# Reading back the first choices' rows in ten loads of two blocks instead of six paired loads, at the end of a graph-attention and expert-layer kernel

## What is computed

```python
gate = jax.nn.softmax(xt @ Wg, axis=-1)
topv, topi = jax.lax.top_k(gate, K)                      # K = 2 of 8 experts
topv = topv / (jnp.sum(topv, axis=-1, keepdims=True) + 1e-06)
...
for e in range(E):
    h = jax.nn.gelu(xt @ W1[e] + b1[e], approximate=False)
    ye = h @ W2[e] + b2[e]
    out = out + ye * scores[:, e:e + 1]
...
x = x + ffn(layernorm(x))
```

## Time and profile before

| | us |
|---|---|
| median of three runs | 1333.1 (1332.76 to 1335.24) |
| the profiled execution, its own time | 1335.91 |
| its span, first to last instruction | 1334.2 |
| busy: PE, DVE, POOL, ACT | 1198.6, 1066.7, 772.1, 696.7 |
| the tiles of the experts | about 1105 to 1306 of the span |
| the sums and their stores | about 1306 to 1334 |

### The profile page before, as it was taken

The page is one execution under the profiler, slowest core; times in us unless marked ns, Lnnn a source line. Parts: engine busy times, 40 slices in busy tenths (PEclk is TensorE's granted clock), DMA queues, the critical chain, the costliest instruction groups (busy, mean ns, idle before and its releaser), DMA issues. The chain is left out here.

```text
span 1334.2 us, 23031 instructions
## 1 busy us (share of the span) xinstructions
PE 1198.6 (90%) x6584; PEld 844.4 (63%) x6585; DVE 1066.7 (80%) x2179; ACT 696.7 (52%) x1198; POOL 772.1 (58%) x859
## 2 busy tenths in 40 slices
PE   6999995999999999999994999999999747999985
PEld 1455554756666666666652888877777535777752
DVE  8999888999999999999988998888888992212216
ACT  5444433988898998989882000000100565555541
POOL 1201006776777777777727777777777704655541
PEclk9999996999999999999995999999999867999988
DMA  9134328998999999999958898888887763343478
GB/s 258 64 127 159 127 96 297 315 296 279 310 310 311 312 309 306 310 301 313 306 150 205 280 314 286 290 293 289 291 271 246 260 229 107 133 134 134 129 272 312
DMA packets 141838, 324.61 MB, mean 243 GB/s; under 512 B 30178, under 2 KB 46294, under 8 KB 141610
## 3 DMA queue, kind: packets, MB, share of 16 engines
q0 software_dynamic: 62816, 212.87, 49.1%
q1 hardware_dynamic: 76842, 109.42, 24.2%
q10 hardware_dynamic: 2080, 1.05, 0.3%
HBM read 257.35 MB, written 65.93 MB: 242 GB/s over the span
## 5 line engine op out<-in xcount | busy, mean ns | idle before, releaser
L1337 PE MATMUL m_ps<-msg,big 128*128 128x260 f32 x1344 | 304.8, 387 | 15.0 <-SPq L1148 14.7
L1337 PEld LDWEIGHTS m_ps<-msg,big 128*128 128x128 f32 x1344 | 254.2, 191 | 65.7 <-issue 27.8
L1188 POOL DMA_INDIRECT big<-he_d,target x234 | 237.5, 1015 | 71.3 <-issue 66.1
L952 PE MATMUL gs_ps<-hrs,hot_t 128*128 x672 | 245.0, 446 | 6.5 <-DVE hot_t L791 4.4
L1261 DVE TENSOR_TENSOR msg<-big 128x512 f32<-128x512 f32 x336 | 213.2, 689 | 40.8 <-DMA big<-he_d,target 39.3
L773 POOL DMA_INDIRECT x_sb<-table_d,target x186 | 192.6, 1035 | 77.0 <-issue 40.7
L1059 ACT ACTIVATE big<-big,raw_a 128x512 f32<-128x512 f32 x264 | 215.4, 816 | 8.8
L804 DVE TENSOR_TENSOR big<-big 128x512 f32<-128x512 f32 x264 | 179.8, 681 | 6.0 <-ACT big L1059 5.6
L1057 ACT ACTIVATE big<-d_ps 128x512 f32<-128x512 f32 x264 | 155.0, 587 | 49.1 <-PE d_ps L972 47.8
L798 DVE TENSOR_TENSOR x_sb<-x_sb,gs_ps 128x512 f32<-128x512 f32 x252 | 169.0, 678 | 14.2 <-PE gs_ps L952 7.3
L972 PE MATMUL d_ps<-ident,x_sb 128*128 128x128 f32 x1008 | 162.3, 284 | 4.1 <-DVE x_sb L798 3.3
(11 more groups left out here) (361 smaller groups left out, 2021.1 us busy)
## 6 DMA issues: line engine op xcount, KB each, us to landing
big<-early_d SPq DMA_DIRECT2D x84, 256.0 KB, 4.3
early_d<-x_sb SPq DMA_DIRECT2D x63, 256.0 KB
x_sb<-local_d SPq DMA_DIRECT2D x84, 128.0 KB, 5.3
big<-in_L_ffn_W_dram SPq DMA_DIRECT2D x16, 512.0 KB
big<-pairs_d SPq DMA_DIRECT2D x6, 1024.0 KB, 10.1
early_d<-big SPq DMA_DIRECT2D x21, 256.0 KB
table_d<-big POOLq DMA_DIRECT2D x10, 520.0 KB, 3.5
both_d<-big POOLq DMA_DIRECT2D x10, 520.0 KB, 4.4
```

The lines of the kernel that those rows point to most:

```text
L952: last = pe.matmul(gs_ps[:, use(n, t) % 3, :], h, hrs[:, bass.ds(blk, 1), piece, :].rearrange("p a f -> p (a f)"), start=(piece == 0), sto ...
L1188: pool.indirect_dma_start(g[:, r, t, :, :, :].rearrange("p c h d -> p (c h d)"), None, he_d, bass.IndirectOffsetOnAxis(ap=k["target"][:, q ...
L1337: last = pe.matmul(m_ps[:, bass.ds(slot[t], 1), j, 0:HEADS // 2 * HW].rearrange("p a f -> p (a f)"), hot[:, r, t, :], halves[:, r, t, j, : ...
```

## The change

The low rows are loaded in nine loads of two blocks and one of one block, and ahead of every load but the first SP waits until the one before has landed. So one of these loads is under way at a time, where there were two. The tail, the high loads, the stores and all other engines keep their instructions and their order.

```diff
-    PARTS = (0, 4, 7, 11, IN_W1, 17, NB - 1)
+    PARTS = tuple(range(0, NB - 1, 2)) + (NB - 1,)
+    assert IN_W1 in PARTS
...
         tiles_stored(0)
         for n in range(len(PARTS) - 1):
-            if n >= 2 and n % 2 == 0:
+            if n >= 1:
                 sp.wait_ge(low_in, lows_landed(n))
             load(low(PARTS[n], PARTS[n + 1]), 0, PARTS[n], PARTS[n + 1], low_in)
         load_tail(low(NB - 1, NB)[0:TAIL, 0, :], 0, low_in)
```

## The result

| | before | after |
|---|---|---|
| median, us | 1333.6 (7 runs) | 1339.78 (7 runs) |
| ratio, 95% interval | | 1.0043, 1.0031 to 1.0055 |
| first low load issued (from the span's start) | 1265.9 | 1263.8 |
| `y` of tile 45 done | 1306.1 | 1296.9 |
| the 26 additions start | 1310.6 | 1313.2 |

The change makes the kernel slower by 4.1 to 7.3 us. One of the seven runs after the change took 3204.78 us; the ratio is taken without it, and the median of the other six is 1339.2. In the two traces the stretch from the first low load to the 26 additions grows by 4.8 us; what lies ahead of it differs by 2.1 us the other way, though nothing was changed there: the kernels of the experiments, which have the same instructions ahead of it, issue that load at 1262.1 to 1269.1 us in their traces. From here on times are compared from the issue of the first low load.

The account below looks back on a forecast made before the run. The start of DVE's 26 additions plus a fixed rest was taken to bound the kernel; high rows move it from 1310.56 to 1313.0, +2.4 us, the tiles' gain hidden: 1335.5 us from 1333.1, range 1329.0 to 1341.0.

Parts of the forecast that it names:

- same: Whole kernel: time within 2.7 us of before, for mean load prices of 3.66 to 4.27 us; chance 0.42.
- the slower rival: Low loads: each stays at 4.5 us even after the gathers, so the end moves +4.8 us to 1337.9; chance 0.38.
- What bounds the end: VectorE's end: the time is the start of the 26 additions, which need tile 45, low rows and high loads, plus a fixed rest.
- The tiles: Expert tiles: smaller backlog cuts gather excess to about 1.1 us; `y` of tile 45 comes 6 to 7 us earlier, but hidden.
- The price of a load: SP's nine waits on 512 KB loads: five at 4.5 us, four at 3.9, tenth load issued 38.1 us after the first.
- High rows: First two high loads, issued at 1304.9: landing taken as 1313.0, which sets the start of the 26 additions.
- one with scatters: First two high loads: 5.5 + 3.3 = 8.8 us as before, landing at 1313.7.
- one at 405 GB/s: First two high loads: 392 KB ahead and their 2048 KB run at 405 GB/s from 1306.2, landing at 1312.4.
- The faster one: Low loads: price nearer 3.5 us, tenth issued at 1297.4, end moves -4.2 us to 1328.9; chance 0.20.
- The form with 3.2 us a load: Stronger faster rival: nine low loads make 28.8 us, end moves by -6.9 us to 1326.2; chance 0.05 of the 0.20.
- the formula quoted for it: Price of one DMA transfer: 2.0 us plus the bytes at 436 GB/s, an estimated 3.2 us for 512 KB.
- At no cost: SP's extra issues, 0.4 us each, lie within waits; PE's lower clock costs little, its last copy 8 us ahead of its store.

Follow-up runs that it names:

- the two kernels on the tail: Changed kernel with the 68-row tail issued ahead of all low loads, 1.004 to before; or in place but split into 64 and 4 rows, 1.0053.

## Why the prediction was right, and where it was off

The range held the time, but the likeliest case did not: I gave "same" 0.42 with +2.4 us, and the kernel is slower by 5.7 (4.1 to 7.3), where the slower rival stood with 0.38 and +4.8. Point by point:

- *What bounds the end* was right: VectorE's 26 additions, started by low and high rows. They take 17.31 us as before.
- *The tiles* came out as forecast: an excess of 1.2 us for a gather (1.1 forecast), no half clock while the tiles run, tile 45 at 33.2 us from the first load (33 forecast). It was hidden, as forecast, since VectorE then waited 10.2 us for rows.
- *The price of a load.* Forecast 4.5 beside gathers and 3.9 after, 38.1 in all; measured 4.57 on average (six of them) and 3.67 (three), 38.6 in all. The mean, 4.29, lay just above 4.27, the border beyond which I had called the forecast wrong. This step gave 0.5 us of the miss.
- *High rows: the step that failed.* "I take 1313.0" put the start 9.0 us after the tenth load's issue; it was 10.9. I had taken the middle of two prices: one with scatters, which left out the 392 KB ahead, and one at 405 GB/s, which let them count by their bytes only. The stretch behind the tenth load moved 192 GB/s, and the tail's 68 rows delayed low and high rows alike, which the two kernels on the tail show for about 1.7 us. The step is off by 1.9 us in all, and with the 0.5 us it makes the forecast's +2.4 the traced +4.8.
- *Rivals.* The faster one fell: no load in the changed kernel cost less than 3.57. The slower one had the right size but mostly another reason: the loads after the gathers did get cheaper, which it denied. The form with 3.2 us a load fell too. The Trainium skill, "DMA: Bandwidth & Descriptors", states the formula quoted for it for transfers issued by GpSimd, which the prediction did not say; these loads are issued by SP.
- *At no cost* held: PE's sums ran partly at the lower clock, and its last copy still came 3 us ahead of its store.

The runs lie 0.9 us above the 4.8 of the two traces, within the interval. For the nine kernels of the experiments, too, the runs lie above what the traces give, by 0.5 to 3.2 us. All are compared with one trace of the kernel before, so its start of 44.7 is probably about 1 us later than is usual for that kernel; no second trace of it shows this.

## What to carry to other kernels

A wait between loads costs each load its part that does not scale with size, here 1.6 to 2 us, and everything behind on the same queue inherits the sum; two small loads under way hid most of that part here and still kept the backlog small. Before protecting a stage from transfers, look at what its result will wait for: here the tiles gained 7 us and VectorE then waited 10 us for the rows. A small load of a partial block can cost more than its bytes when it stands right ahead of what is waited for, as the 68 rows did here.

## What the runs showed of the hardware that I had not expected

- A gather is not held up for as long as a backlog lasts: with 5 MB of loads issued freely it took at most 7.2 us, with pairs of 1792 KB 8.1, with loads of 512 KB one at a time 5.2, and before the loads began 3.1 to 3.5.
- 136 KB in 68 rows, ahead of the high loads, put off the landing of the first two (2 MB) by 1.7 us (9.53 against 7.84 us), and 0.9 us of this went away when the same bytes came as 64 and 4 rows. Both are counted from the issue of the second high load.
- The same load of two blocks beside the same tiles took from 4.05 to 5.34 us in one execution.
